# One program per engine, four token tiles normalised inside the first attention, and new buffer addresses, in a gated cross-attention kernel in split fp32

## The reference, cut to what matters

```python
x = x + tanh(g_xattn[0]) * xattn0(layernorm(x), ctx)   # 32 heads of 128, 8 kv heads, biases, softmax over 64 keys
x = x + tanh(g_ffn[0])   * ffn0(layernorm(x))          # silu(x Wg^T) * (x Wu^T), 1376 wide, then W_down
x = x + tanh(g_xattn[1]) * xattn1(layernorm(x), ctx)   # keys = [ctx, x] (64 + 256), RMS norm on q and k, no biases
x = x + tanh(g_ffn[1])   * ffn1(layernorm(x))          # x base^T + top-2 of 28 experts, each of rank 8
```

## Time and profile before

| | |
|---|---|
| median of 3 runs | 1425.98 us (1424.87 to 1427.61) |
| profiled execution | 1427.87 us, its span 1426.1 us |
| granted TensorE clock, mean | 0.994 of full speed |
| TensorE busy | 97% of the span, 7976 matmuls and transposes |
| DVE, ACT, POOL busy | 73%, 56%, 36% |
| DMA | 63.82 MB, 45 GB/s on the mean |

### The profile page before, as it was taken

The page is one execution under the profiler, slowest core; times in us unless marked ns, Lnnn a source line. Parts: engine busy times, 40 slices in busy tenths (PEclk is TensorE's granted clock), DMA queues, the critical chain, the costliest instruction groups (busy, mean ns, idle before and its releaser), DMA issues.

```text
span 1426.1 us, 23791 instructions
## 1 busy us (share of the span) xinstructions
PE 1377.5 (97%) x7976; PEld 1195.4 (84%) x7976; DVE 1040.2 (73%) x2732; ACT 799.9 (56%) x2216; POOL 506.6 (36%) x626
## 2 busy tenths in 40 slices
PE   6999999999999998999999999999999999999998
PEld 5899998987778876888888888888888888888877
DVE  7777777787623337787788788787778778778775
ACT  6788777774211315565565565556556555656631
POOL 5865556654955612222222212122222221222220
PEclk8999999999999999999999999999999999999999
DMA  5221122211321300100101001001001001000001
GB/s 201 73 75 60 58 74 74 74 60 60 105 60 47 127 0 1 74 1 3 72 1 48 26 0 74 0 0 74 0 0 74 0 0 74 15 30 14 1 9 52
DMA packets 14942, 63.82 MB, mean 45 GB/s; under 512 B 1760, under 2 KB 1760, under 8 KB 10656
## 3 DMA queue, kind: packets, MB, share of 16 engines
q1 hardware_dynamic: 14880, 63.07, 12.5%
HBM read 60.97 MB, written 2.10 MB: 44 GB/s over the span
## 4 chain that ended last, share of the span: by engine, by line
PE 55%; DVE 5%; ACT 2%; issue 1%; POOL 0%; DVEq 0%; ACTq 0%
PE psum L57 16%; PE psum L59 15%; PE psum L58 15%; PE psum L1436 3%; PE psum L1447 2%; PE psum L1468 2%; PE psum L1431 1%; DVE w1q_lo L1054 1%; DVE v_lo L1133 1%; DVE pT_hi L1065 1%; PE psum L1544 1%; DVE pT_lo L1061 0%; ACT p L1302 0%; DVE dump L1125 0%; PE psum L120 0%
## 5 line engine op out<-in xcount | busy, mean ns | idle before, releaser
L1302 ACT ACTIVATE p<-psum,nb,rq 128x320 f32<-128x320 f32 x256 | 155.4, 614 | 149.4 <-DVE nb L1100 149.4
L1021 POOL TENSOR_TENSOR p<-p,rinv 128x640 f32<-128x640 f32 x64 | 80.2, 1253 | 203.6 <-DVE rinv L1106 203.6
L57 PE MATMUL psum<-w1q_hi,xnT_lo 128*128 128x512 f32 x288 | 120.2, 417 | 10.0 <-DVE v_lo L1133 7.3
L59 PE MATMUL psum<-w1q_hi,xnT_hi 128*128 128x512 f32 x288 | 114.0, 396 | 0.0
L58 PE MATMUL psum<-w1q_lo,xnT_hi 128*128 128x512 f32 x288 | 112.9, 392 | 0.0
L1096 DVE TENSOR_REDUCE mx<-psum 128x2 f32<-128x640 f32 x128 | 104.8, 819 | 3.4 <-PE psum L59 1.3
L1061 DVE TENSOR_TENSOR pT_lo<-psum,pT_hi 128x512 fp32r<-128x512 f32 x128 | 85.2, 687 | 28.4 <-ACT pT_hi L1279 26.9
L1279 ACT ACTIVATE pT_hi<-psum 128x512 fp32r<-128x512 f32 x128 | 69.6, 597 | 60.4 <-PE psum L1436 60.4
L57 PE MATMUL psum<-w1o_hi,oT_lo 128*128 128x512 f32 x256 | 100.4, 392 | 0.0
L58 PE MATMUL psum<-w1o_lo,oT_hi 128*128 128x512 f32 x256 | 100.3, 392 | 0.0
L59 PE MATMUL psum<-w1o_hi,oT_hi 128*128 128x512 f32 x256 | 99.7, 389 | 0.0
(11 more groups left out here) (235 smaller groups left out, 4645.0 us busy)
## 6 DMA issues: line engine op xcount, KB each, us to landing
raw_q<-in_w0q SPq DMA_DIRECT2D x8, 1024.0 KB, 4.8
raw_o<-in_w0o SPq DMA_DIRECT2D x8, 1024.0 KB, 4.8
raw_q<-in_w1q SPq DMA_DIRECT2D x8, 1024.0 KB, 7.5
raw_o<-in_w1o SPq DMA_DIRECT2D x8, 1024.0 KB, 4.9
raw_kv<-in_w_gu SPq DMA_DIRECT2D x10, 512.0 KB, 3.6
raw_gu<-in_w_gu SPq DMA_DIRECT2D x10, 512.0 KB, 3.6
raw_kv<-in_w0kv SPq DMA_DIRECT2D x8, 515.0 KB, 3.3
raw_kv<-in_w1kv SPq DMA_DIRECT2D x8, 512.0 KB, 5.5
```

What stands on the lines that cost most here:

```text
L57: pe.matmul(out, w[1], m[0], start=start, stop=False)
L59: return pe.matmul(out, w[0], m[0], start=False, stop=stop)
L1021: pool.tensor_tensor(p, p, k.rinv[:, stat(j)].unsqueeze(2).to_broadcast([PART, 2, KEYS]), ALU.mult).then_inc(p_scaled_pool, 1)
L1302: last = act.activation(k.p1[:, tile, 2 * hp + hh, :], s_pair(j)[:, hh, :], ACT.Exp, bias=k.nb[:, i:i + 1], scale=k.rq[:, i:i + 1], accum_ ...
```

## The change

**Head and group 0.** `EARLY = 4`: only tiles 0 to 3 are turned in the head, with two WK pieces for each of the first three. Tile 4 + s is turned within step s of group 0, after the scores of tile s, through `o_bank`; its statistics, normalisation and splits stand in the lists of DVE, ACT and POOL at the same steps. Scores of tile s wait for `ln.split` s + 1. Of w0o, POOL splits two pieces in the head and two in t = 0 and 1 of the group; `split_kv(1)` moves from the start of the group to t = 3, and the kv fill from s = 3 to s = 4. The load of w0o goes ahead of the last two loads of x.

**Bias.** The addition of `gbo` to `x` goes from group 0 to the last group (table `BIAS`), `gbo` is made after `body(0)`.

**One program.** The phases return their five functions, and one Block calls the three of each engine one after the other. The second chunk of the FFN is loaded by SP in the first attention, its first chunk's low part is made at t = 4, the gate and up banks are swapped, and waits are added where a Block's end stood.

**FFN and second attention.** The high parts of `w_down` go to ACT and the low parts to DVE, one by one (table `DOWN`). DVE splits the queries' weights of group 0 in the FFN's last step. The low parts 2 and 3 of w1q are made in the unit b = 3, ahead of and behind `scale_p(n, 2)`, after the two `x_add`.

**Addresses.** Alignment 256 bytes for all but small tensors; `w_kv`, `kT1`, `WK` and the key half of `kvT` start 48 words behind a multiple, `ctxT` 32 words; `w_gu0` is a view of the `w_kv` buffer that starts at its multiple. `kvT` becomes two pairs, and `w0q`, `w0o`, `WK`, `kvT` are allocated ahead of the rest.

```diff
@@ first attention
+    EARLY = 4
+    def steps_fills(s, nxt, first=False):
+        own, more = OWN_PREP.get(s, []), NEXT_PREP.get(s, []) if nxt else []
+        if first and s == 3:
+            return own
+        if first and s == 4:
+            return NEXT_PREP[3] + own + more
+        return own + more
+    def late_tile(s, first):
+        return first and EARLY + s < NT
+    def late_bank(s):
+        return o_bank[s % 2]
@@ SP
+            if i == 2:
+                weights("o")
-        weights("o")
...
+        sp.wait_ge(prep_full, HEAD + FILLS * (NKV - 2) + ORDER.index(("wk", 7)) + 1)
+        k.ffn0_gate_up(sp, 1)
@@ POOL, body
+        BIAS = {0: [0, 1, 2], 1: [3, 4], 2: [5, 6], 3: [7]}
-                split_kv(g + 1, 2 if first else HEAD + FILLS * (g - 1) + ORDER.index(("kv", 1)) + 1)
+            if nxt and not first:
+                split_kv(g + 1, HEAD + FILLS * (g - 1) + ORDER.index(("kv", 1)) + 1)
...
+                if first and t < 2:
+                    split_o(t + 2)
+                    ln.pool_rstd(pool, 0, EARLY + 1 + t)
+                if first and t == 3:
+                    split_kv(1, 2)
...
+                if first and t == 1:
+                    ln.pool_rstd(pool, 0, NT - 1)
-                elif t == 2:
+                if not nxt and t == 4:
                     k.ffn0_w_lo(pool, 0)
...
-                if isinstance(g, int) and g == 0:
-                    pool.tensor_tensor(k.x[:, t, :], k.x[:, t, :], k.gbo[:, :], ALU.add).then_inc(bo_added, 1)
+                for m in BIAS.get(t, []) if not nxt else []:
+                    pool.wait_ge(x_done, NT * (NKV - 2) + m + 1)
+                    pool.tensor_tensor(k.x[:, m, :], k.x[:, m, :], k.gbo[:, :], ALU.add).then_inc(bo_added, 1)
@@ POOL, head
-        for t in range(NT):
+        for t in range(EARLY):
             ln.pool_rstd(pool, 0, t)
...
+        split_o(0)
+        ln.pool_rstd(pool, 0, EARLY)
+        split_o(1)
@@ PE, body and head
+                    if first:
+                        pe.wait_ge(ln.split, s + 1)
...
+                if late_tile(s, first):
+                    ln.pe_turn(pe, 0, EARLY + s, late_bank(s))
...
-                if not nxt and s == 6:
-                    pe.wait_ge(prep_free, base + OWN)
+                if not nxt and s in (6, 7):
+                    pe.wait_ge(prep_free, base + OWN + s - 8)
...
-        pe.wait_ge(ln.split, NT)
@@ first FFN
-    gate_bank, up_bank, o_bank = [k.bank[0], k.bank[2]], [k.bank[1], k.bank[3]], k.bank[4:8]
+    gate_bank, up_bank, o_bank = [k.bank[2], k.bank[0]], [k.bank[3], k.bank[1]], k.bank[4:8]
+    DOWN = {0: [0, 1], 1: [2, 3], 2: [4], 3: [5], 4: [6], 5: [7], 6: [8], 7: [9], 8: [10]}
@@ POOL
-                if n < IC - 1:
-                    dn(n)
-                if n == IC - 2:
-                    dn(IC - 1)
@@ DVE
+            p, raw = slice(0, width(i)), down_raw(i)
+            dve.wait_ge(dn_hi, i + 1)
+            dve.tensor_tensor(k.w_dn[1][p, i, :], raw, f(k.w_dn[0][p, i, :]), ALU.subtract).then_inc(dn_lo, 1)
...
+            for m in DOWN.get(n, []):
+                dn(m)
...
+            if n == len(STEPS) - 1:
+                k.attn1_split_q(dve)
@@ ACT
+            act.wait_ge(dn_in[j], 16 * len(dn_slices(*DN[j][1:])))
+            act.activation(k.w_dn[0][p, i, :], down_raw(i), ACT.Copy).then_inc(dn_hi, 1)
@@ PE
+            if n < 2:
+                pe.wait_ge(ln.split, NT + 4 + n)
@@ second attention, DVE
-                    if b == 0 and not first:
-                        w_lo("q", g, 2)
-                        w_lo("q", g, 3)
...
                     x_add(u, b, 0)
+                for c in conv[4:5]:
+                    w_lo(*c)
                 scale_p(n, 2)
                 if prev:
                     x_add(u, b, 1)
+                for c in conv[5:6]:
+                    w_lo(*c)
...
-                w_lo("q", NKV, 2)
-                w_lo("q", NKV, 3)
@@ PE
+            if not prev:
+                pe.wait_ge(k.f0_x_done, NT - 1)
@@ build
+CTX_SHIFT, SHIFT = 32, 48
...
+        def sb(scope, name, shape, dtype=F32, align=256):
+            return scope.enter_context(nc.sbuf_tensor(name, [PART] + shape, dtype, align_bytes=align))
+        def small(scope, name, shape):
+            return sb(scope, name, shape, align=64)
...
+        k.ctxT = pair(stack, "ctxT", [CH * BATCH * CTX], CTX_SHIFT)
+        w_kv = [sb(stack, "w_kv" + part, [SHIFT + KVW], F32R) for part in ("_hi", "_lo")]
+        k.w_kv, k.w_gu0 = [w[:, SHIFT:] for w in w_kv], [w[:, 0:KVW] for w in w_kv]
+            k.WK = pair(scope, "WK", [CH, BATCH, GH, CTX], SHIFT)
+            k.kvT = [pair(scope, "kT0", [BATCH * CTX], SHIFT), pair(scope, "vT0", [BATCH * CTX])]
+    k.kT = pair(scope, "kT1", [BATCH, CTX + SEQ + CTX], SHIFT)
```

More of the change, by code:

```diff
@@ L384, in body @@
         def body(g, nxt):
-            base = HEAD + FILLS * g
+            base, first = HEAD + FILLS * g, isinstance(g, int) and g == 0
             for s in range(NT + 3):
@@ L483, in body @@
         def body(g, nxt):
-            base = HEAD + FILLS * g
+            base, first = HEAD + FILLS * g, isinstance(g, int) and g == 0
             for s in range(NT + 3):
                 n = NT * g + s
-                for fill in steps_fills(s, nxt):
+                for fill in steps_fills(s, nxt, first):
                     if fill[0] == "kv" and fill[1] == 0:
@@ L490, in body @@
                     prep(base, fill, nxt)
+                if late_tile(s, first):
+                    ln.act_hi(act, 0, EARLY + s, late_bank(s))
                 if 2 <= s < NT + 2:
@@ L616, in body @@
                         pe.wait_ge(prep_free, place(base, ("vw", 3, 1), nxt)[0] + 1)
-                    if not (first and t < 2):
+                    if first and t < 2:
+                        pe.wait_ge(ln.split, NT - 1 + t)
+                    else:
                         pe.wait_ge(x_done, n - 4)
@@ new lines, in sync, with gpsimd @@
+    def sync(sp):
+        for n in range(2, len(STEPS)):
+            k.ffn0_gate_up(sp, n)
+            if n == 6:
+                k.ffn0_down(sp, 2)
+        sp.wait_ge(dn_lo, IC)
+        k.attn1_load(sp, "q")
+        k.attn1_load(sp, "o")
+        sp.wait_ge(gu_wlo, len(STEPS) - 1)
+        k.attn1_load(sp, "kv")
+    def gpsimd(pool):
+        for n, (half, i) in enumerate(STEPS):
+            if n + 2 < len(STEPS):
+                k.ffn0_w_lo(pool, n + 2)
+            p = slice(0, width(i))
+            pool.wait_ge(h_hi, n + 1)
+            pool.tensor_tensor(k.hT[1][p, i, :], k.f_h[p, n % 2, :], f(k.hT[0][p, i, :]), ALU.subtract).then_inc(h_lo, 1)
+            if ln_tiles(n):
+                ln.pool_rstd(pool, *ln_tiles(n)[:2])
+        for t in (4, 5):
+            ln.pool_rstd(pool, 2, t)
@@ new lines, in build, with _ @@
+        with nc.Block() as block:
+            @block.sync
+            def _(sp):
+                a0[0](sp)
+                f0[0](sp)
+                a1[0](sp)
+            @block.gpsimd
+            def _(pool):
+                a0[1](pool)
+                f0[1](pool)
+                a1[1](pool)
+            @block.vector
+            def _(dve):
+                a0[2](dve)
+                f0[2](dve)
+                a1[2](dve)
+            @block.scalar
+            def _(act):
+                a0[3](act)
+                f0[3](act)
+                a1[3](act)
+            @block.tensor
+            def _(pe):
+                a0[4](pe)
+                f0[4](pe)
+                a1[4](pe)
```

1534 lines of the change are left out of this document (749 added, 785 removed).

## The result

The changed kernel takes 1413.08 us (median of four runs, 1411.80 to 1413.97) against 1426.80 (1424.87 to 1428.98) for the kernel before: ratio 0.9904, 95% interval 0.9891 to 0.9916. It is faster by 13.7 us where 32.1 were forecast, and lies outside the range of 1386 to 1406. The profiled execution took 1413.25 us, its span is 1411.4 against 1426.1.

A forecast was written before the change was run, and what follows sets the result against it. TensorE was taken as the bound in steady groups, with the remaining idle at the seams. Eight parts summed to 32.1 us, taken from the median 1426.0 to give 1393.9 us, range 1386 to 1406.

The forecast's parts named there:

- Part 1: Head and first attention group: four fewer tiles turned in the head let the first scores start near 26 us; -4.5 us.
- Given back: Losses within Part 1: tile turns inside the group +1.7 us, POOL's late split of the kv weights +1.0 us.
- Rival 3: POOL bounds the first group with w0o pieces, chains and kv in series; Part 1 gives nothing, 1398.4 us; chance 0.12.
- Part 2: Bias addition moves from first to last attention group, covered by scalings wanted later; counted 0, up to 2 us without cover.
- Part 3: New operand start addresses bring matmuls closer together: w_kv -5.7, kT -5.0, ctxT -1.0 us; 11.7 us in all.
- rival 1: The 320-column matmuls gain nothing from the new start addresses; 1398.9 us; chance 0.17.
- Parts 4 and 6: Seams into the FFN (-2.5 us) and into the second attention (-1.8 us): waits at the blocks' ends go.
- Part 5: FFN's first half: w_down split leaves POOL (-3.6 us), waits for late weights go; -5.0 us, ends -2 and -6.
- Part 7: Second attention: query weights' low parts made a unit earlier, cutting TensorE's v_lo wait; -4.1 us, ends -1 and -8.
- 0.8 each: Gain in us at each of seven new groups in Part 7, before TensorE's own speedup there is taken off.
- Part 8: Tail: two low parts no longer hold the first base projection, half clock may go; -2.5 us, ends -1 and -4.4.
- rival (2): No start address matters, or the allocator gives other offsets; 11.7 us less gain, 1405.6 us; chance 0.09.

## Why the prediction was wrong

**What bounds the kernel** held: TensorE's rate in steady state, idle time at the seams.

**Part 1, forecast -4.5, measured +1.0.** The first scores came at 26.8 (forecast 26), a wait for the second w0o piece in place (2.02). The failed step is "Given back": I counted POOL's work in the group against the time TensorE needs, a sum, and got +1.0 for w_kv. What decided is the place in the list: two pieces behind a `wait_ge(p_rec)`, the wait for a tile's probabilities, 3.9 us of waits on TensorE, and the lower clock that follows two of the three waits of the stage. The run on POOL's order gives 5.0 back with the same work, some 4.3 of it by the order. Rival 3 named the engine and the series, but for it part 1 gives nothing; a loss was left out, though the waits could have been estimated from the earlier trace rows and the new list. The +1.0 is of two single executions: head and group 0 took 73.01 us in the kernel before with the new addresses, against 74.44, and 74.05 to 75.50 in the six profiled executions that have the change's lists there. The 4.5 is in none of them.

**Part 2, forecast 0, up to 2.** The wait of 1.42 us stands where 1.03 was before, so the three additions cost 0.4. Nearly right. The cover I named did not hold for the first additions, and the room on POOL lies elsewhere: it idles 8.25 us ahead of the first scaling.

**Part 3, forecast -11.7, measured 0 (-1.7 to +2.1 by the interval of the run with the addresses alone).** This is the step that failed most. That a distance goes by the difference of the starts was right for the two rows and is shown by the series; the inferences from it were not. The 320 columns gain nothing in 48 series (rival 1), and in the second attention kT even lost 0.35 us in six groups. The price of a pair is not fixed by the pair: 113.3 and 117.8 both occur at a difference of 192, and the kernel fell on 117.8 for most of w_kv. WK, priced at no change, lost 2.2 ns on 768 matmuls. And the 512 columns, priced at 0 because they "stay at multiples", lost 0.85 us with pT and v. I had two rows at one width, and spread them over 1800 matmuls. Beside it, the Trainium skill (TensorE: Matmul & The Clock Gate, Back-to-back issue gap) would have N/2.4 + 2.5 ns at every start; by it part 3 is worth 0, which the total happens to be, as a balance of gains and losses. The trace does not agree with its reason: over N/2.4 the least here is 6.6 ns at 256 columns and 13.4 at 320 and 512, and the start moves it.

**Parts 4 and 6, forecast -2.5 and -1.8**, measured -2.0 (with the 0.4 of part 2 in it) and -2.0 (the FFN's second half with its seam, 94.8 us to 92.8): right in the step and in the size, the waits marked as PEq and the 0.65 ahead of the first tile turn. The run with three Blocks brings 3.8 us of these waits back; the rest of its 7.5 is nearly all clock.

**Part 5, forecast -5.0, measured -6.0** (the FFN's first half, 97.6 us before, 91.5 after). The run with the old split of w_down gives 5.1 of it to the split; the late second chunk (0.93 us in the earlier trace rows) is the rest. On the rule in the Trainium skill (SBUF — State Buffer, Who interferes with whom) the trace agrees in kind: POOL's hT_lo takes 1.70 us on the mean beside DVE's new low parts, 1.44 in the same steps before the change and 1.29 in the second half. Against the second half that is 3.7 us on POOL in nine steps, half of the 7.1 worked out there, and POOL is no longer the bound.

**Part 7, forecast -4.1, measured -2.4.** The term mis-sized is "0.8 each": 1.2 less 0.5 plus 0.1. A unit with a turnover went from 27.3 us to 27.05, 0.3 each. The wait of the earlier trace rows went, but another of 0.9 us for v_lo's first part came at each turnover. The 0.5, by which the second low part pushes the row maximum and the exponentials, was too small: ACT waits for that maximum 2.25 us, against 1.40 with the two low parts on POOL, and v_lo comes behind it. On POOL they bring 1.1 of the 1.2. Whether another order of DVE's list would do as well was not tried.

**Part 8, forecast -2.5, measured -3.6**, within its ends. The wait of 2.65 us gave way to one of 1.08 for pT_lo, 1.6 gained where 1.5 was forecast, and the lower clock behind it (granted 0.59 from 1361.88 to 1366.00 us before) did not come again, where I had counted it as possible.

The prices of rivals (2) and (3) came together: each alone was inside the range (1405.6, 1398.4), both are 1410, and part 7 fell short besides. Their reasons held only in part. Start addresses do matter, against rival (2), and its number came by a balance that nobody forecast; and POOL bounded the first group by its order, not by its work. The chances named only one rival at a time, so that two at once had no place in them.

## What to carry to other kernels

When work moves into a busy stage, write out each queue's list with the time at which its waits are satisfied; a sum of busy times says nothing of a piece that stands behind a wait. A distance between matmuls read from one pair of buffers is not a price for others: measure it over widths, starts and what runs before, in one program of its own, before counting it a thousand times. A wait that goes is followed by the next one on the list: look at what that engine had in front of it. And before a difference of a microsecond or two between two profiles is given to an edit, see where the granted clock fell in each.

## What the runs showed of the hardware

The distance between back-to-back fp32r matmuls depends on the difference of the operands' starts modulo 256 bytes, in opposite directions at 256 and 512 columns (120.0 against 113.3 ns, 226.7 against 233.3) and not at 320 (146.7), and at 256 columns with a difference of 64 or 192 it takes one of two values (113.3 or 117.8) for a series. This is from one program on zeroed buffers. What picks the value was not found.

A wait of TensorE of about 2 us is followed by the lower clock in some executions and not in others, at the same place of the same order. The head's wait of 1.99 to 2.03 us stands in eight profiled executions; the lower clock came at its end, or within 1.2 us of it, in six, and not in the run on POOL's order and in that with the query's low parts on POOL. The wait for w_kv_lo near 45 us was 2.02 to 2.07 us long in five executions and had none behind it in any. All six waits of 2.40 to 2.93 us had one within 1.8 us. Why some of the shorter ones have it was not found.
